# Computing the q part of the gates inside the value projection, instead of in a tiled product of its own

## The reference

```python
x = x + mlstm(layernorm(x), ctx, ctx, ...)     # q = layernorm(x); k = v = ctx; 4 heads of 64
x = x + ternary_linear(layernorm(x))
x = x + cross_attention(layernorm(x), ctx)
x = x + ternary_ffn(layernorm(x))

# inside mlstm:
if_in = concatenate([q, k, v], axis=-1)                    # 3 * 256 features
ig = einsum('bsf,hf->bsh', if_in, igate_w) + igate_b       # 4 input gates per row
fg = einsum('bsf,hf->bsh', if_in, fgate_w) + fgate_b       # 4 forget gates per row
# log_sigmoid(fg), a cumulative sum and a running maximum give the matrix D
C = (q_h @ k_h.T / 8) * D
h = C / max(|sum(C)|, exp(-max_log_D)) @ v_h, then normalised per head
```

## Time and profile before

| | |
|---|---|
| runs of the kernel | 709.58 us median of 3 (708.42 to 710.64) |
| the profiled execution | 709.58 us |
| its span, first to last instruction | 707.6 us |
| busy: TensorE | 655.3 us, 93% |
| busy: VectorE | 604.7 us, 85% |
| busy: ScalarE | 522.5 us, 74% |
| busy: GpSimd | 395.9 us, 56% |
| mean granted TensorE clock | 0.978 |
| the chain that ended last | TensorE 49%, VectorE 37%, ScalarE 7% |

### The profile page before, as it was taken

The page is one execution under the profiler, slowest core; times in us unless marked ns, Lnnn a source line. Parts: engine busy times, 40 slices in busy tenths (PEclk is TensorE's granted clock), DMA queues, the critical chain, the costliest instruction groups (busy, mean ns, idle before and its releaser), DMA issues.

```text
span 707.6 us, 15589 instructions
## 1 busy us (share of the span) xinstructions
PE 655.3 (93%) x4958; PEld 494.6 (70%) x4958; DVE 604.7 (85%) x1655; ACT 522.5 (74%) x1203; POOL 395.9 (56%) x556
## 2 busy tenths in 40 slices
PE   4877999999999999999999999986899999999996
PEld 3656887877877878878778778764366666666664
DVE  4698688898898898898988988986699999999994
ACT  3455668777877879787778787764688888888985
POOL 2165555745745656557447465541366666666665
PEclk9998999999999999999999999987799999999999
DMA  8301022022121220230211211005232433434321
GB/s 289 100 1 61 3 88 91 16 91 74 48 91 46 75 90 17 92 98 22 91 66 56 90 45 47 31 28 167 60 83 79 122 103 90 128 82 142 94 80 60
DMA packets 72653, 55.46 MB, mean 78 GB/s; under 512 B 20093, under 2 KB 72318, under 8 KB 72582
## 3 DMA queue, kind: packets, MB, share of 16 engines
q1 hardware_dynamic: 64134, 50.37, 23.1%
q10 hardware_dynamic: 8448, 4.20, 2.0%
HBM read 29.39 MB, written 20.97 MB: 71 GB/s over the span
## 4 chain that ended last, share of the span: by engine, by line
PE 49%; DVE 37%; ACT 7%; issue 5%; DMA 1%; POOL 0%; DVEq 0%; POOLq 0%; ACTq 0%
PE bank L655 10%; PE bank L569 8%; PE bank L620 8%; PE bank L599 7%; DVE st L1096 6%; DVE C L1357 5%; PE bank L672 4%; DVE hmax L1360 4%; DVE x L1319 3%; DVE x L1292 3%; PE bank L664 2%; ACT x2T L767 2%; DVE hh L1288 2%; PE bank L528 2%; DVE mv L1099 2%
## 5 line engine op out<-in xcount | busy, mean ns | idle before, releaser
L655 PE MATMUL bank<-WGU,fqT 128*128 128x512 bf16 x512 | 127.1, 388 | 4.7 <-DVEq L1334 2.7
L992 POOL TENSOR_SCALAR_AFFINE_SELECT D<-D 128x512 f32<-128x512 f32 x64 | 38.5, 638 | 115.8 <-ACT D L819 115.8
L977 POOL TENSOR_TENSOR rs<-ve,minus_half 128x4 f32<-128x4 f32 x64 | 64.4, 1013 | 64.8 <-DVE ve L1102 64.6
L655 PEld LDWEIGHTS bank<-WGU,fqT 128*128 128x128 bf16 x512 | 48.8, 99 | 60.2 <-DVE C L1357 16.2
L1357 DVE SCALAR_TENSOR_TENSOR C<-bank,fback,D 128x1024 f32<-128x1024 f32 x64 | 82.1, 1283 | 9.8 <-ACT D L906 6.1
L906 ACT ACTIVATE D<-bank,fback 128x1024 f32<-128x1024 f32 x64 | 71.3, 1114 | 19.4 <-PE bank L655 19.4
L1360 DVE TENSOR_REDUCE hmax<-C 128x1 f32<-128x1024 f32 x64 | 78.1, 1220 | 2.2
L910 ACT ACTIVATE fhT<-bank 128x1024 f16<-128x1024 f16 x64 | 65.5, 1024 | 16.3 <-PE bank L664 15.3
L1048 POOL TENSOR_SCALAR wtmp<-C,hscale 128x1024 f32<-128x1024 f32 x64 | 71.8, 1122 | 0.2 <-issue 0.2
L1096 DVE BATCH_NORM_STATS2 st<-x 128x6 f32<-128x256 f32 x192 | 67.2, 411 | 2.9
L672 PE MATMUL bank<-WD,fhT 128*128 128x256 f16 x512 | 66.3, 273 | 0.3 <-ACT fhT L910 0.3
(11 more groups left out here) (188 smaller groups left out, 1499.7 us busy)
## 6 DMA issues: line engine op xcount, KB each, us to landing
out_dram<-x SPq DMA_DIRECT2D x32, 512.0 KB, 3.2
xg<-in_x_dram SPq DMA_DIRECT2D x16, 512.0 KB, 3.9
cg<-in_ctx_dram SPq DMA_DIRECT2D x16, 512.0 KB, 4.5
rows_q<-fq ACTq DMA_DIRECT2D x16, 256.0 KB, 2.2
xg<-out_dram SPq DMA_DIRECT2D x8, 512.0 KB, 4.6
cg<-out_dram SPq DMA_DIRECT2D x8, 512.0 KB, 4.7
raw<-in_L_ffn_w_gate_dram SPq DMA_DIRECT2D x1, 1024.0 KB, 8.6
x<-in_L_ffn_w_up_dram SPq DMA_DIRECT2D x1, 1024.0 KB, 11.1
```

Of the source, the lines that this page charges most:

```text
L655: mm = pe.matmul(ps[k + half], fqT[:, s, c, :], WGU[:, c, which, half * 512:(half + 1) * 512], start=(c == 0), stop=(c == EC - 1))
L977: pool.tensor_tensor(rs[i][:, :], ve[i][:, :], minus_half[:, 0:GB], ALU.pow).then_inc(rstd[i], 1)
```

## The change

The q part of the gates becomes part of VG. In each of the four batches, behind the two f32 matmuls of the ctx part, two more use the q blocks of qcT as stationary operand and the 8 columns of WGQ as moving operand, and add into columns 256 to 263 of the same bank. `gate_rows`, the stage GQ, `gate_turned`, the transpose and `gate_q` go; the bias is spread over all partitions in the setup, as 8 columns, and VectorE adds it in the gate sum. VG now waits for the copies of TX as well.

```diff
-FIRST = uses(("TC", "TX", "GQ", "VG", "KQ", "GT", "GA", "WS", "TA"))
+FIRST = uses(("TC", "TX", "VG", "KQ", "GT", "GA", "WS", "TA"))
...
-        WGQ = sb("WGQ", [P, EC, 32])
-        gate_bias = sb("gate_bias", [P, 1])
-        gate_turned = sb("gate_turned", [P, P])
-        gate_q = sb("gate_q", [P, GB, 2 * NH])
+        WGQ = sb("WGQ", [P, EC, 2 * NH])
+        gate_bias = sb("gate_bias", [P, 2 * NH])
...
-            pe.matmul(ps[7][:, 0:1], brow_at[:, :, :].rearrange("o b g -> o (b g)"), ones[0:1, 0:1], start=True, stop=True)
+            pe.matmul(ps[7][:, 0:8], ones[0:1, :], brow[:, :], start=True, stop=True)
...
-                def gate_rows(o):
-                    for i in range(GB // 2):
-                        moved("TX", i)
-                    for c in range(EC):
-                        for b in range(GB):
-                            mm = pe.matmul(o[32 * b:32 * b + 32, 3 * P:4 * P], WGQ[:, c, :], qcT[p][:, c, b, :],
-                                           start=(c == 0), stop=(c == EC - 1), skip_group_check=True)
-                    return mm
...
                     if stage == "VG":
...
                         for b in range(GB):
                             o = open_("VG", b)
                             moved("TC", b // 2)
+                            moved("TX", b // 2)
                             for c in range(EC):
-                                mm = pe.matmul(o[:, 0:VG], qcT[p][:, EC + c, b, :], WX[:, c, :],
-                                               start=(c == 0), stop=(c == EC - 1))
-                            if b == GB - 1:
-                                moved(*(("GQ", 0) if "GQ" in bank.stages else half(b)))
-                                mm = pe.transpose(o[:, 3 * P:4 * P], gate_turned[:, :], ident[:, :])
+                                pe.matmul(o[:, 0:VG], qcT[p][:, EC + c, b, :], WX[:, c, :],
+                                          start=(c == 0), stop=False, skip_group_check=True)
+                            for c in range(EC):
+                                mm = pe.matmul(o[:, E:E + 2 * NH], qcT[p][:, c, b, :], WGQ[:, c, :],
+                                               start=False, stop=(c == EC - 1), skip_group_check=True)
                             shut(mm, "VG", b)
...
-                            if b == GB - 1 and n is not None:
-                                mm = gate_rows(o)
                             shut(mm, *half(b))
...
-                        u = act.activation(usq[:, b, :, :], v[:, :, 0:DH], ACT.Square)
-                        if b == GB - 1 and n is not None:
-                            u = turned_gates(o)
-                        u.then_inc(done, 1)
+                        act.activation(usq[:, b, :, :], v[:, :, 0:DH], ACT.Square).then_inc(done, 1)
...
-                    v = act.activation(vg[r][:, b, :], o[:, 0:VG], ACT.Copy)
-                    if b == GB - 1:
-                        v = act.activation(gate_q[:, :, :], o[:, 3 * P:4 * P].rearrange("p (b g) -> p b g", g=32)[:, :, 0:2 * NH],
-                                           ACT.Copy)
-                    v.then_inc(done, 1)
+                    act.activation(vg[r][:, b, :], o[:, 0:VG], ACT.Copy).then_inc(done, 1)
...
-            pool.memset(brow_at[:, :, :], 0.0)
-            pool.memset(WGQ[:, :, :], 0.0)
...
-            dve.wait_ge(sel0, 1)
-            dve.tensor_copy(brow_at[:, :, 0:2 * NH], brow[:, :].unsqueeze(1).broadcast_to([1, GB, 2 * NH]))
...
-                    dve.tensor_tensor(gates[:, :, :], vg[r][:, :, E:E + 2 * NH], gate_q[:, :, :], ALU.add).then_inc(gstep, 1)
+                    dve.tensor_tensor(gates[:, :, :], vg[r][:, :, E:E + 2 * NH],
+                                      gate_bias[:, :].unsqueeze(1).broadcast_to([P, GB, 2 * NH]),
+                                      ALU.add).then_inc(gstep, 1)
```

More of the change, by code:

```diff
@@ L41 @@
 WEIGHTS = {"W0", "WG", "WU", "WD"}
-USES = {"KQ": 2, "GT": 1, "TB": 1, "TC": 2, "TX": 2, "UA": 2, "UB": 2, "TA": 1, "GA": 1, "GQ": 1, "MB": 1, "WS": 1, "W0": 1, "WG": 2, "WU": 2,
+USES = {"KQ": 2, "GT": 1, "TB": 1, "TC": 2, "TX": 2, "UA": 2, "UB": 2, "TA": 1, "GA": 1, "MB": 1, "WS": 1, "W0": 1, "WG": 2, "WU": 2,
         "WD": 2}
@@ L132, in build @@
         brow = sb("brow", [1, 2 * NH])
-        brow_at = sb("brow_at", [1, GB, 32])
         orow = sb("orow", [1, E])
@@ L558, in turn @@
                         shut(mm, "GT")
-                    if stage == "GQ":
-                        pe.wait_ge(wcopy, 2)
-                        shut(gate_rows(open_("GQ")), "GQ")
                     if stage == "VG":
                         if isinstance(n, int) and n == 0:
+                            pe.wait_ge(wcopy, 2)
                             pe.wait_ge(wload[6], 16)
@@ L699, in _ @@
             for c in range(EC):
-                act.activation(WGQ[:, c, 0:2 * NH], ps[6][:, 8 * c:8 * c + 8], ACT.Copy, scale=8.0)
+                act.activation(WGQ[:, c, :], ps[6][:, 8 * c:8 * c + 8], ACT.Copy, scale=8.0)
                 a = act.activation(WX[:, c, E:E + 8], ps[6][:, 16 + 8 * c:24 + 8 * c], ACT.Copy)
@@ L703, in _ @@
             act.wait_ge(wpe, 2)
-            act.activation(gate_bias[:, :], ps[7][:, 0:1], ACT.Copy)
+            act.activation(gate_bias[:, :], ps[7][:, 0:8], ACT.Copy)
             act.activation(head_scale[:, :], ps[7][:, 128:128 + E], ACT.Copy, bias=1.0).then_inc(wcopy, 1)
@@ L751, in last_rows @@
                     store_rows(NG - 1)
-            def turned_gates(o):
-                return act.activation(gate_turned[:, :], o[:, 3 * P:4 * P], ACT.Identity, bias=gate_bias[:, 0:1])
             def turn(bank, n, m, z, y, w, p, r):
@@ L837, in turn @@
                     half_copies("TX", 0)
-                if starting:
-                    o, done = filled("GQ")
-                    turned_gates(o).then_inc(done, 1)
                 if m is not None:
```

## The result

The changed kernel takes 716.75 us in the median of four runs (715.96 to 718.27), the kernel before 709.41 us (708.42 to 710.64). The ratio is 1.012, with a 95% interval from 1.010 to 1.0141: slower by 7.3 us. The forecast was 724.2 us with a range from 716 to 731, so the direction and the range held, the range by 0.75 us, and the size was twice too large: 14.6 us were forecast. The execution that was profiled took 717.83 us and has a span of 716.1 us, 8.5 us more than before.

A forecast was written before the change was run, and what follows sets the result against it. Bound: one closed chain of waits per 27.85 us turn, through TensorE's VG. The profiled 709.6 us, plus 14.0 for 14 turns at +1.0 and 0.6 for the first turn, gave 724.2 us, range 716 to 731.

The forecast's parts named there:

- The path through VG: Steady loop: VG lies on the chain of waits in 14 turns of 27.85 us, so added TensorE time there moves the turn.
- The price of a short matmul: VG: each of 16 8-column instructions per turn costs one full f32 weight load, 0.108 us, together 1.73 us.
- Rival A: VG: short matmuls' weight loads hide under the long streams, 0.22 us a turn; 700.5 us, faster; chance 0.08.
- the generous reading of the Trainium skill's window: VG: all four loads of a batch hide under its long streams, leaving about 25 ns per matmul, 0.40 us a turn.
- Rival B: VG: each short instruction costs 0.165 us, as at L587, 2.64 us a turn; 736.8 us; chance 0.06.
- What was removed: Per turn, gate instructions (0.57 us) and transpose (0.12) leave TensorE's path, gate_q's copy (0.09) ScalarE's; gate_turned's copy was off the chain.
- I cost this gain at nothing: UB's earlier signal lets hvar and VectorE run about 0.9 us sooner, but this becomes a wait ahead of the gate sum.
- From hh on nothing changes: Steady loop: hh starts 1.0 us later per turn and everything behind it keeps its length, 14 x 1.0 = +14.0 us.
- F0's wait stays: TensorE's 0.58 us wait ahead of F0, released by VectorE work behind hh, remains.
- rival C: Loop: VectorE's 1.16 us wait or TensorE's 0.58 us ahead of F0 absorbs the longer TensorE stretch; about 710.2 us; chance 0.04.
- The first turn: Removed work gives −1.47 us, 16 short matmuls cost 1.73 to 2.49; taken as +0.6 us.
- The second turn: TensorE idles 6.42 us behind VG, waiting for nlf; one more microsecond vanishes in that, so 0.

The follow-up runs named there:

- tiled version: Kernel before with its tiled gate product moved from behind UB's last product into the bank of VG's first batch: 702.9 us, ratio 0.9928.
- second trace of the changed kernel: The changed kernel run once more, unedited, against the kernel before: 718.67 us, ratio 1.0144.

## Why the prediction was right or wrong, step by step

**The path through VG** was right: VG is in the chain of the changed loop, the turn moved with it, and without the short matmuls the kernel falls to 698.09 us.

**The price of a short matmul** was nearly right. Forecast 16 x 0.108 = 1.73 us a turn, measured 5.37 − 3.81 = 1.56, 0.098 each. A group of four behind long matmuls takes 0.34 us and makes the next long ones 0.05 longer (1.01 instead of 0.96); only behind other short ones does a group cost 0.45, 0.112 each. That the columns don't set it is shown, since eight times as many change nothing; that the weight load does is the reading that is left. Rival A, with loads hidden under the long streams, is refuted, and with it the generous reading of the Trainium skill's window ("TensorE: Matmul & The Clock Gate", Part 2); the short matmuls are not hidden. Rival B's 0.165 us is refuted too.

**What was removed** came off the path as forecast: 0.57 and 0.12 us. With VG's true length the last vg copy starts 0.86 us later, where the forecast had +0.95 to +1.04 for the work behind it. ScalarE is 6.9 us less busy (522.5 and 515.6 us), where some 9 had been named.

**"I cost this gain at nothing"** is the step that failed. The sooner signal of UB, and hvar without its wait for gate_turned, were to end as VectorE's wait ahead of the gate sum. The wait came (1.09 us, where about 1.5 had been named), but VectorE wasn't the only one that ran sooner: hv released GpSimd's power, and GpSimd's vaug came sooner behind it. From F0's start vaug now ends at 16.03 us instead of 17.82, and it met other VectorE work. This changed the turn in two places. Ahead of hh, the stretched gate operations moved hh by 0.38 us more than VG did. Behind hh 0.59 us came back. By its own signs the prediction was wrong here: hh moved by 1.24 us and VG's end by 0.86, and F0's wait didn't stay.

**"From hh on nothing changes", and F0's wait stays** failed with it. I had read the 0.58 us ahead of F0 as VectorE's own work, and so gave rival C's absorbing 0.04. Part of that VectorE work was stretched beside GpSimd: 0.30 us on x1, beside vaug, and 0.32 on the last ve, beside D. Once it wasn't, TensorE's longer stretch had 0.59 us to grow into. Rival C was therefore true for more than half a microsecond a turn, by a mechanism that neither it nor the forecast named. The two runs that move only vaug in the changed kernel show it in both directions: 710.48 us with vaug out of the way, 722.45 with it late. The run with UB's earlier signal in the old orientation, 702.9 us, shows the gain without the short matmuls. Where vaug is moved by GpSimd's order, the power hr moves too: in the kernel before this cost more than it gave (714.27 us), and so it did on top of the tiled version (707.35 against 702.9).

**The sum.** In the profiled execution 13 turns add 370.06 − 361.92 = 8.1 us and the last 1.2, about 9.4 us instead of 14.0. With 0.3 behind the loop and the setup's −1.2 that is the span's 8.5; the medians differ by 7.3. That the time stayed inside the range is in part luck: the bound of 716 us stood for short matmuls at 0.07 us, and they took 0.098; what brought the time near it were F0's wait, which was taken up, and the setup. **The first turn**, +0.6, is neither confirmed nor refuted, since the setup scatters by more. **The second turn** at 0 was right in the second trace of the changed kernel, whose chain passes through VectorE's work there. In the first trace VG ran at the low clock and was on the chain, nlf ended 0.3 us later than before, and TensorE waited for it only 0.56 us.

The meeting of vaug and VectorE has a rule in the Trainium skill ("SBUF — State Buffer", "Who interferes with whom"): VectorE instructions with two SBUF inputs contend with a GpSimd instruction that reads SBUF, as those in a two-port mode do with GpSimd, for one shared pair of ports, and whoever comes first holds it for its whole instruction. The rows agree for vaug: the gate operations take 0.47 to 0.68 us beside it, about one vaug piece (2.33 us for four, 0.58 each), though alone they take 0.17 to 0.20; the row maxima, a reduction from PSUM, take 0.87 us for four beside vaug, in the kernel before, and 0.88 without it, in the changed one. They don't agree for the power hr, which reads SBUF too: in the kernel before it runs from 135.47 to 138.37 us, and the gate sum inside it takes 0.18 us. There the measurement decides. Applied to vaug, the rule would have named the step that the forecast missed.

## What to carry to other kernels

When an edit frees one engine sooner, follow the release further, to the engine behind it: its next instructions move too, and may start to collide, or cease to collide, with work on the path. Here a matmul instruction of 8 columns cost as much as one of 64, 0.098 us on average, and one of the tiled product 0.036. So before turning such a product round, keep the small matrix on the stationary side, in column groups side by side, and look for a cheaper place for its result; that was worth 0.7%. And a wait of TensorE for VectorE is not yet VectorE's own length; compare the same instruction's duration in two places or kernels (1.22 against 1.52 us here) before calling it slack or bound.

## What the runs showed of the hardware that was not expected

- VectorE's tiny operations (128x16 to 128x96) took 0.17 to 0.20 us alone and 0.47 to 0.68 beside GpSimd's 128x256 subtraction; x1 took 1.22 and 1.52 us, the scan 0.42 and 0.83. GpSimd paid as well: four subtractions took 2.33 us beside the gate operations, 3.40 and 4.36 beside hh and x1.
- GpSimd's power (hr, 2.90 us) had no such effect on the VectorE work beside it: in the run with vaug first the gate operations beside it took 0.17 to 0.20 us, and in the kernel before too (0.18 to 0.20).
- Four f32 matmul instructions of 8 columns and four of 64 columns behind long ones take the same time, a batch of 1.35 us. A second group of four behind the first takes 0.45 us, where the first takes 0.34.
- The granted clock fell to 0.50 (1.2 GHz) at about 40 us in one execution of the changed kernel and at 56 us in another, with the same program; the time of the first F0 differed by 1.9 us between them.
